# Delta of a Mamba block from one Softplus function instead of a sum of parts, with the loops written out

## What is computed

```
dt, Bm, Cm = split(xc @ Wx)                     # xc: convolved, through silu
delta = softplus(dt @ Wdt + bdt)                # softplus(v) = log(1 + exp(v))
A = -exp(A_log)
h = exp(delta * A) * h + (delta * xc) * Bm      # the scan over time, 16 states per channel
y = sum over states of h * Cm, plus xc * Dp
x = x + (y * silu(z)) @ Wblk
```

## Time and profile before

| | us |
|---|---|
| median of 3 runs | 2144.67 |
| the 3 runs | 2141.48, 2144.67, 2146.16 |
| span of the profiled execution | 2143.5 |
| VectorE busy | 1943.2 |
| TensorE busy | 1877.8 |
| ScalarE busy | 1683.8 |
| POOL busy | 1458.1 |

### The profile page before, as it was taken

How to read it: one execution, slowest core, us unless ns; L and a number is a source line. 1 busy time by engine, 2 the same in 40 slices (tenths; PEclk the granted TensorE clock), 3 DMA queues, 4 the chain that set the end, 5 groups by cost and what they waited for, 6 DMA issues and landing times.

```text
span 2143.5 us, 34659 instructions
## 1 busy us (share of the span) xinstructions
PE 1877.8 (88%) x10816; PEld 1183.1 (55%) x10816; DVE 1943.2 (91%) x1826; ACT 1683.8 (79%) x3053; POOL 1458.1 (68%) x1364
## 2 busy tenths in 40 slices
PE   4788888888888888888888888888888799999998
PEld 1444444444444444444444445444444499989998
DVE  3799999999999999999999999999999987767775
ACT  4899999899999998989999999999999433333333
POOL 2688888888888888888888988888889600000000
PEclk9899999999999999999999999999999999999999
DMA  7323232323232323232333333332322200000000
GB/s 241 86 64 79 63 78 62 78 62 78 62 79 63 80 65 79 64 79 65 81 78 73 81 76 79 78 78 62 78 62 72 84 1 11 11 12 11 11 6 11
DMA packets 72786, 138.55 MB, mean 65 GB/s; under 512 B 13072, under 2 KB 31120, under 8 KB 68112
## 3 DMA queue, kind: packets, MB, share of 16 engines
q1 hardware_dynamic: 66320, 119.28, 22.7%
q10 hardware_dynamic: 6400, 18.42, 3.7%
HBM read 63.85 MB, written 7.74 MB: 33 GB/s over the span
## 4 chain that ended last, share of the span: by engine, by line
ACT 27%; PE 26%; POOL 26%; issue 13%; DVE 6%; ACTq 1%; SPq 1%; DMA 1%; POOLq 0%; DVEq 0%
POOL scan L478 12%; POOL scan L472 11%; PE y_ps L1291 11%; ACT decay L563 10%; PE dbu_ps L1266 8%; ACT scan L641 6%; DVE scan L829 3%; POOL scan L469 2%; PE dbu_ps L1067 2%; ACT sp_e L600 2%; ACT delta L601 2%; ACT sp_l L610 2%; PE y_ps L1052 2%; ACT sp_e L605 1%; ACT du_t L626 1%
## 5 line engine op out<-in xcount | busy, mean ns | idle before, releaser
L829 DVE TENSOR_TENSOR_SCAN scan<-decay,dbu_ps 128x1024 f32<-128x1024 f32 x512 | 1154.6, 2274 | 29.8 <-PE dbu_ps L1067 21.9
L1067 PE MATMUL dbu_ps<-ident,scan 128*128 128x128 f32 x4096 | 571.6, 286 | 220.7 <-DVE scan L829 195.9
L478 POOL TENSOR_TENSOR scan<-scan,c_rep 128x1024 f32<-128x1024 f32 x255 | 671.8, 2635 | 130.4 <-ACT du_t L626 66.5
L1067 PEld LDWEIGHTS dbu_ps<-ident,scan 128*128 128x128 f32 x4096 | 482.2, 147 | 500.1 <-DVE scan L829 259.3
L563 ACT ACTIVATE decay<-d_rep,a_cur 128x510 f32<-128x510 f32 x1024 | 668.0, 709 | 54.1 <-POOL scan L478 15.7
L472 POOL TENSOR_SCALAR scan<-du_t,b_t 128x256 f32<-128x256 f32 x896 | 594.8, 679 | 0.0
L641 ACT ACTIVATE scan<-du_t,b_t 128x256 f32<-128x256 f32 x1024 | 445.6, 494 | 1.2
L838 DVE TENSOR_TENSOR scan<-scan,c_rep 128x1024 f32<-128x1024 f32 x257 | 331.0, 1288 | 0.0
L766 ACT ACTIVATE decay<-dbu_ps 128x512 f32<-128x512 f32 x256 | 147.9, 597 | 205.2 <-PE dbu_ps L1266 183.1
L1052 PE MATMUL y_ps<-scan,sel 128*32 128x512 f32 x2048 | 299.8, 661 | 0.0
L1080 PE MATMUL pre_ps<-xn,w_pre 128*128 128x512 f32 x512 | 245.5, 603 | 5.2 <-DVE w_pre L818 5.2
(11 more groups left out here) (110 smaller groups left out, 1648.8 us busy)
## 6 DMA issues: line engine op xcount, KB each, us to landing
d_rep<-delta SPq DMA_DIRECT2D x496, 128.0 KB, 2.9
c_rep<-c_rows SPq DMA_DIRECT2D x32, 1024.0 KB
w_pre<-prepared_weights ACTq DMA_DIRECT2D x15, 866.0 KB, 13.0
prepared_weights<-scan SPq DMA_DIRECT2D x3, 1122.0 KB, 12.9
scan<-in_conv_w SPq DMA_DIRECT2D x4, 512.0 KB, 5.0
w_out<-prepared_weights SPq DMA_DIRECT2D x16, 128.0 KB, 12.5
sp_e<-in_x_rows SPq DMA_DIRECT2D x8, 256.0 KB, 3.2
d_rep<-in_w ACTq DMA_DIRECT2D x2, 1024.0 KB, 6.8
```

The lines of the kernel that those rows point to most:

```text
L478: nc.gpsimd.tensor_tensor(ring[slot % RING], ring[slot % RING], c_rep[par][:, slot // PRS, :].unsqueeze(1).broadcast_to([128, 2, TG]), ALU ...
L829: nc.vector.tensor_tensor_scan(ring[slot % RING].rearrange("p u t -> p (u t)"), decay[slot % DEC].rearrange("p u a t -> p (u a t)"), dbu_p ...
L1067: last = nc.tensor.transpose(dbu_ps[slot % 2][:, u, 128 * j:128 * j + 128], dbu_t[m % 2][:, j, b, :, :].rearrange("p q c -> p (q c)"), ide ...
```

## The change

ScalarE makes delta with the function Softplus, straight from the PSUM bank with the bias, one instruction for each half, in slot 7. Softplus is in a table of its own, so the kernel asks for that table ahead of it and for the one with Exp and Ln behind it. The Abs, Relu, Exp, Square and Ln of ScalarE and the three instructions of VectorE go, with their semaphores. What waited for `dt_used` now waits for `half_delta` (after the first half) or `delta_ready` (after the second); what waited for `sp_ready` waits for `delta_ready`. Apart from that, `windows` and `group_pairs` are Python loops, so that every window and every group is written out and no engine has a loop.

```diff
-        def windows(eng, window):
-            window(-1, -1, 1)
-            for s in (0, 1):
-                window(s, 0, s)
-            with eng.Fori(1, PAIRS - 1) as i:
-                for par in (0, 1):
-                    window(2 * i + par, i, par)
-            for s in (STEPS - 2, STEPS - 1):
-                window(s, PAIRS - 1, s % 2)
-            window(STEPS, PAIRS, 0)
+        def windows(window):
+            for s in range(-1, STEPS + 1):
+                window(s, s // 2, s % 2)
...
-        def group_pairs(eng, stage_fn):
...
+        def group_pairs(stage_fn):
+            for g in range(GROUPS):
+                stage_fn(g, g // 2, g % 2)
...
-            def softplus_parts(s):
+            def softplus(s):
+                nc.scalar.preload_act_table_set("softplus")
                 wait(act, du_ready, s)
                 for k in range(KT):
                     act.wait_ge(dt_ready, 2 * s + k + 1)
-                    bias = w_pre[:, W_DB + k:W_DB + k + 1]
-                    bank = pre_ps[1 - k][:, :]
-                    nc.scalar.activation(sp_e[:, k, :], bank, ACT.Abs, bias=bias)
-                    nc.scalar.activation(delta[:, k, :], bank, ACT.Relu, bias=bias).then_inc(dt_used, 1)
-
-            def softplus_logs(s):
-                act.wait_ge(dt_used, 2 * s + 2)
-                nc.scalar.activation(sp_e[:, :, :], sp_e[:, :, :], ACT.Exp, scale=-1.0).then_inc(act_sp, 1)
-                act.wait_ge(act_sp, s + 1)
-                wait(act, dut_mm, 2 * s)
-                nc.scalar.activation(sp_w[:, :, :], sp_e[:, :, :], ACT.Square, scale=LOG_SCALE,
-                                     bias=log_bias[:, :])
-                nc.scalar.activation(sp_l[:, :, :], sp_e[:, :, :], ACT.Ln, bias=one[:, :])\
-                    .then_inc(sp_ready, 1)
+                    nc.scalar.activation(delta[:, k, :], pre_ps[1 - k][:, :], ACT.Softplus,
+                                         bias=w_pre[:, W_DB + k:W_DB + k + 1]).then_inc((half_delta, delta_ready)[k], 1)
+                load_exp_and_ln()
...
                     if slot == 7 and has(s, 1):
-                        softplus_parts(s + 1)
+                        softplus(s + 1)
                     if slot == 8 and has(s, 1):
-                        softplus_logs(s + 1)
                         if par == 0 and has(s, 2):
-                            act.wait_ge(sp_ready, s + 2)
+                            act.wait_ge(delta_ready, s + 2)
...
-                    if has(s, 1):
-                        if slot == 8:
-                            dve.wait_ge(sp_ready, s + 2)
-                            nc.vector.scalar_tensor_tensor(out=sp_w[:, :, :], in0=sp_w[:, :, :], scalar=LOG_ADD,
-                                                           in1=sp_e[:, :, :], op0=ALU.add, op1=ALU.mult)\
-                                .then_inc(dve_sp, 1)
-                            dve.wait_ge(dve_sp, 2 * (s + 1) + 1)
-                            nc.vector.scalar_tensor_tensor(out=sp_l[:, :, :], in0=sp_l[:, :, :], scalar=LN_ERROR,
-                                                           in1=sp_w[:, :, :], op0=ALU.add, op1=ALU.min)\
-                                .then_inc(dve_sp, 1)
-                            dve.wait_ge(dve_sp, 2 * (s + 1) + 2)
-                            nc.vector.tensor_tensor(delta[:, :, :], delta[:, :, :], sp_l[:, :, :], ALU.add)\
-                                .then_inc(delta_ready, 1)
...
             def turn_b(s):
-                pe.wait_ge(dt_used, 2 * s + 1)
+                pe.wait_ge(half_delta, s + 1)
...
                 if has(s, 2):
-                    pe.wait_ge(dt_used, 2 * (s + 3))
+                    pe.wait_ge(delta_ready, s + 3)
```

More of the change, by code:

```diff
@@ L36 @@
 EPS = 1e-5
[L40 to L43, removed]
 JT = TG // 128
@@ L101, in build_program @@
         eps = sb("eps", [128, 1])
-        one = sb("one", [128, 1])
-        log_bias = sb("log_bias", [128, 1])
         bout_rep = sb("bout_rep", [128, DM])
@@ L214, in build_program @@
         dt_ready = sem("dt_ready")
-        dt_used = sem("dt_used")
         bt_mm = sem("bt_mm")
@@ L218, in build_program @@
         skip_done = sem("skip_done")
-        act_sp = sem("act_sp")
-        sp_ready = sem("sp_ready")
-        dve_sp = sem("dve_sp")
+        half_delta = sem("half_delta")
         delta_ready = sem("delta_ready")
@@ L406, in window @@
                             .then_inc(w2_loaded[e // half], 16)
-            windows(sp, window)
+            windows(window)
             out_rows = out.rearrange("a s d -> (a s) d")
@@ L421, in finish @@
                              stage[par].rearrange("p (j d) -> p j d", j=JT)).then_inc(out_done[par], 16)
-            group_pairs(sp, finish)
+            group_pairs(finish)
             for par in (0, 1):
@@ L510, in _ @@
             normalise(0)
-            windows(pool, window)
+            windows(window)
             def prepare_next(g, i, par):
@@ L515, in prepare_next @@
                     add_bout(g + 1, i if par == 0 else i + 1, 1 - par)
-            group_pairs(pool, prepare_next)
+            group_pairs(prepare_next)
         @block.scalar
@@ L767, in relu @@
                         .then_inc(relu_ready, 1)
-            windows(act, window)
+            windows(window)
             def experts(g, i, par):
@@ L785, in experts @@
                             route(g + 1)
-            group_pairs(act, experts)
+            group_pairs(experts)
             root_ff(GROUPS - 1, 1)
@@ L792, in _ @@
             nc.vector.memset(eps[:, :], EPS)
-            nc.vector.memset(one[:, :], 1.0)
-            nc.vector.memset(log_bias[:, :], LOG_BIAS)
             nc.vector.memset(mean_w[:, :], 1.0 / DM)
@@ L1003, in square @@
                                             ALU.mult).then_inc(h2_ready, 1)
-            windows(dve, window)
+            windows(window)
             def experts(g, i, par):
@@ L1032, in experts @@
                 stats_of(g, 1, acc[par])
-            group_pairs(dve, experts)
+            group_pairs(experts)
             norm2(GROUPS - 1, 1, out_done[1], 16 * (GROUPS // 2 - 1))
@@ L1294, in down @@
                 last.then_inc(down_ready, 1)
-            windows(pe, window)
+            windows(window)
             def experts(g, i, par):
@@ L1311, in experts @@
                 down(g, EXPERTS - 1)
-            group_pairs(pe, experts)
+            group_pairs(experts)
 def is_first(g, e):
```

## The result

| | us |
|---|---|
| changed kernel, median of 4 runs (2156.54 to 2160.7) | 2158.61 |
| kernel before, median over the same runs | 2144.47 |
| ratio, with its 95% interval | 1.0063 (1.0049 to 1.0078) |
| span of the profiled execution of the changed kernel | 2154.8 |

What follows compares the result with a forecast made beforehand. The prediction took ScalarE's own program as the bound and summed 46.5 + 7.5 + 6 + 2.2 = 62.2 us off the 2143.5 us span; with 1.2 us to the median, it forecast 2082 us, range 2030 to 2125.

Steps and rivals of the forecast that it cites:

- What bounds the kernel now: Scan windows: ScalarE's own program, including its z wait, sets the 51.3 us window; VectorE is full but has room.
- ScalarE, what goes and comes: Per window, 5.44 us of instructions go; two Softplus and two table loads cost 3.94: 1.50 less, 46.5 us over 31 windows.
- The w_pre issue: Every second window: ScalarE's issue of the w_pre load can lie under a running decay, 0.5 us each, 7.5 in all.
- Who waits for delta: POOL, PE and d_rep get delta sooner, d_rep earlier only in odd windows; none on ScalarE's cycle, cost zero.
- I take this wait as fixed: ScalarE's z wait, 2.33 us, ending 19.3 us after its du_t copy via POOL and PE, was assumed not to change.
- The signs of being wrong: For the transfer rival: a PE wait for w_pre or a decay wait for d_rep in every second window.
- (c): Rival: a transfer replaces what goes; w_pre priced, 2 us lost in each of 15 window pairs, 2112 us; chance 0.18.
- The start: Serial stretch before the first window: delta 7.5 us sooner, d_rep 5.8 sooner behind c_rep; 6 us gained.
- Straight loops: Expert loop's back edge: PE's 2.23 us idle goes, once; nothing gained at the window loop's back edges.
- Rival (b): Loop branches cost 2.2 us at each of 13 back edges, hidden in waits: 29 us more, 2054; chance 0.05.
- The sum: Whole kernel: 46.5 + 7.5 + 6 + 2.2 = 62.2 us saved, forecast 2082 us.
- (d): Rival: table switches around Softplus cost more than they save, four loads instead of two, 2171 us; chance 0.10.

Runs made afterwards that it cites:

- e6: Changed kernel with c_rep in four DMAs and ScalarE's copy of du_t in slot 13 instead of 14: 2013.0 us, ratio 0.9389.
- e8: Kernel before, delta still made of parts, with all loops written out and c_rep in four DMAs: 2125.2 us, ratio 0.9911.
- e7: Changed kernel with c_rep in four DMAs, Relu in place of Softplus and no table switches around it: 2015.6 us, ratio 0.9401.
- e4: Changed kernel with d_rep issued only once c_rep has landed: 2159.0 us, ratio 1.0079.
- e3: Changed kernel with c_rep loaded in four DMAs of 32 partitions each instead of one: 2118.8 us, ratio 0.9892.
- e5: e3 with PE repeating half of the next convolution projection in slot 15, to stay at work ahead of the next window: 2076.3 us, ratio 0.9683.
- e1: Kernel before, delta still made of parts, with all loops written out: 2128.9 us, ratio 0.9945.
- e12: Kernel before with only the windows written out and the expert loop kept: 2135.9 us, ratio 0.9969.
- e10: Changed kernel with the copy of du_t in slot 13 and c_rep still in one DMA: 2148.6 us, ratio 1.0043.

## Why the prediction was wrong, point by point

**What bounds the kernel now**: half right. ScalarE's own program with the wait on the way copy, POOL, PE, z Silu is a cycle, and e6 shows it: shortened, it takes the time with it. But I looked for who waits longest, and so did not see a second chain without slack that no one waited for: ScalarE's dbc in slot 5, c_rep, d_rep, the next window's first decay. Before, d_rep was over at 773.9 and ScalarE's first decay started at 774.01. It cost next to nothing there (e8: 4 us), but it left no room for a shorter window, and the time from c_rep's issue to there, 27.9 us, was the number to read. I had read the share of the DMA engines only for the w_pre load.

**ScalarE, what goes and comes**: right, 3.99 against 3.94 us, and 2.85 against 2.80 for the two loads (e7). The 2.66 us for a switch that the Trainium skill gives ("ScalarE: Activation LUTs", section "What ACT_TABLE_LOAD costs") is not what the changed kernel shows: 1.28 and the next decay behind it.

**The w_pre issue**: right in that it lies under the table load; no run separates what that gave.

**Who waits for delta**: the step that failed. I wrote that d_rep's transfers come earlier, in odd windows only, at no cost, and that what goes on VectorE and PE is on nobody's cycle. They come earlier in both kinds of window, counted from c_rep: 7.6 us instead of 15.7 behind it in the odd one, 13.0 instead of 15.8 in the even one. d_rep came to lie on top of c_rep, and in e4 its start could be moved by 11 us with no effect. That collision cost 40 us (e3). And the gap of 4.54 us in PE's work did not vanish: PE now idles 2.60 us behind POOL, in front of the transposes that ScalarE's z waits for, with a half-speed clock behind it. That cost 42.5 us (e3 against e5). I had it in the rows: the transposes behind the old gap took 1.32 for 1.09. "I take this wait as fixed" was the sentence in which it was lost; that way from the copy to the z Silu is 19.3 us only while PE's clock holds and POOL's pair takes 0.94 us. The signs of being wrong that I had named for (c) are the ones that showed: ScalarE waits for d_rep and PE for w_pre.

**The start**: d_rep was issued at 36.23 instead of 42.04, as forecast, and the gain was lost in the first window: the second window's Silu load stands at 116.63, before at 116.42. ScalarE waits 13.1 us for d_rep there, which lies behind c_rep too; in e3 the same load stands at 101.31. Of those 15 us the straight loops alone give 5 (111.17 in e1), so the start was worth 10 us and not 6, once c_rep was quick.

**Straight loops**: mis-sized, 2.2 forecast and 13 measured (e1). I looked for gaps at the back edges; about half of the gain lies in the windows, 51.2 us each instead of 51.5 (e1), and the rest is open. Rival (b), 2.2 us at every back edge of the windows, would have given 29 us more, and the windows gave 7 (e12).

**The sum.** Forecast -62. In its place: straight loops -13 (e1 against before), the collision of c_rep and d_rep +40 (changed against e3), the clock +42.5 (e3 against e5). The measured +14 lies 76 us above the forecast, and 40 + 42.5, less the loops' extra 11, is 72; 4 us are left, about what the sessions differ by. The 40 and the 42.5 are steps in the order in which they were removed: e10 shows that with c_rep slow little can be had from the second place, and to fill PE's gap with c_rep slow was not tried. Without the last two terms the kernel stands at 2076 (e5), near the 2082 of the sum. The window, 49.75 us, is the one forecast (49.8); that the total comes so near is in part luck, since the loops' 11 us and the start's 4 beyond the forecast are in it, and against them stand POOL's slower pair and whatever of the smaller terms did not come, which no run separates. Rival (c), a transfer in place of what goes, had the kind of mechanism right and named the wrong transfer: I priced w_pre and only the even windows, 2112. PE did wait for w_pre in the changed kernel too, 26.1 us in all. The rival that ended slower, (d), named the table loads; they cost what was forecast (e7) and are not the cause.

## What to carry to other kernels

When an engine is freed and the profile shows no wait for something, ask for how long it could still be late: read the time from a transfer's issue to its last packet and to its first use, and count what lies ahead of it in the same queue. A gap that is removed can open again elsewhere, and where PE idles next its clock may fall; look who stands behind that place. Then move the copy or the issue that heads the new longest chain: one slot earlier was worth 106 us here, once the transfers had been spread over all engines. The kernel that does both beats both kernels of this study, 2013.0 us against 2144 and 2159. And judge a change again when the next bound has been moved: the same Softplus cost 25 to 30 us before that and saved 112 after it.

## What the runs showed of the hardware

- One DMA whose pattern has four rows outermost kept 0.25 of the DMA engines busy for about 15.7 us per MB; the same bytes in four DMAs with 32 rows outermost took 0.98 of them and about 5 us (e3).
- A second transfer issued 7.6 us behind the slow one ended 32.6 us after the slow one's issue, issued 15.7 behind it after 27.8 (one window of each kernel).
- After 2.60 us without work PE's granted clock was at 0.50 of full speed, 1.2 GHz, for some 3 us (e3); after 0.49 us in the same place it stayed at 2.4 GHz (e6).
- A switch of the activation table took 1.28 us, 64 times more in the run than before, with the next instruction directly behind it; a DMA issue of ScalarE's queue can lie under it.
- POOL's 128x256 products (L452) took 0.47 us, or 1.43 to 1.53, in e3. All 124 long ones had VectorE's 128x1024 product with C (L805) beside them for at least 1.09 us; all 677 that had none of it beside them were short. This was seen and not tested.
